# One power per half step, the third accumulator's load moved forward, and another order on TensorE around the verdict

## The reference

```
x = x + tanh(g0) * attention(layernorm(x), ctx, ctx)
h = layernorm(x)                                   # first feed-forward, 1024 wide
z = h @ ternary(W_syn).T + b_syn
hidden = where(z >= 102nd largest z of the row, relu(z), 0)
x = x + tanh(g1) * layernorm2(h + hidden @ ternary(W_out).T + b_out)
kv = k * v ; y = causal convolution of kv with a 256-long kernel, + D * kv
x = x + tanh(g2) * sum over i of y[i, j] * layernorm(x)[i]     # 16 heads of 8
n = layernorm(x)                                   # second feed-forward
x = x + tanh(g3) * (top-6-of-64 expert mixture(n) + shared expert(n))
```

## Time and profile before

| what | value |
|---|---|
| three timed runs | 716.46 us median (712.61 to 722.75) |
| the profiled execution | 720.17 us, of which the span is 718.4 us |
| mean granted TensorE clock of the span | 0.944 |
| busy: PE, PEld, DVE, ACT, POOL | 611.0, 470.5, 471.6, 296.9, 451.8 us |
| chain that ended last, by engine | PE 57%, DVE 14%, issue 11%, POOL 9%, DMA 6% |

### The profile page before, as it was taken

How to read it: one execution, slowest core, us unless ns; L and a number is a source line. 1 busy time by engine, 2 the same in 40 slices (tenths; PEclk the granted TensorE clock), 3 DMA queues, 4 the chain that set the end, 5 groups by cost and what they waited for, 6 DMA issues and landing times.

```text
span 718.4 us, 11813 instructions
## 1 busy us (share of the span) xinstructions
PE 611.0 (85%) x3072; PEld 470.5 (65%) x3072; DVE 471.6 (66%) x1596; ACT 296.9 (41%) x657; POOL 451.8 (63%) x512
## 2 busy tenths in 40 slices
PE   4789998769788798989857879999999999999920
PEld 2455554446566677877746668888888888878710
DVE  5898987999259988898895534444454454544515
ACT  3157777958233454555455223322233232323200
POOL 2697845782022287878787724777777777786560
PEclk9799999989899999999989899999999999999965
DMA  7579715869959943953333768999999999996878
GB/s 243 181 255 317 258 46 186 231 181 304 317 195 376 373 160 130 309 203 115 150 109 129 237 217 209 240 284 256 281 249 284 258 263 278 264 271 105 231 122 295
DMA packets 97822, 163.69 MB, mean 228 GB/s; under 512 B 10848, under 2 KB 65568, under 8 KB 96736
## 3 DMA queue, kind: packets, MB, share of 16 engines
q1 hardware_dynamic: 76864, 135.16, 56.9%
q0 software_dynamic: 20608, 27.82, 20.2%
q10 hardware_dynamic: 288, 0.01, 0.0%
HBM read 91.24 MB, written 71.71 MB: 227 GB/s over the span
## 4 chain that ended last, share of the span: by engine, by line
PE 57%; DVE 14%; issue 11%; POOL 9%; DMA 6%; ACT 1%; SPq 1%; DVEq 0%; POOLq 0%; ACTq 0%
PE psum L1164 12%; PE psum L1177 7%; PE psum L1168 6%; PE psum L904 5%; POOL xs_rows L781 5%; PE psum L1182 4%; PE psum L1148 4%; PE psum L1048 3%; PE psum L978 3%; PE psum L946 3%; PE psum L947 3%; PE psum L948 2%; DMA acc<-hh,toki 2%; POOL acc L847 2%; DVE Z L1962 1%
## 5 line engine op out<-in xcount | busy, mean ns | idle before, releaser
L847 POOL DMA_INDIRECT acc<-hh,toki x128 | 187.9, 1468 | 80.4 <-DVE hh L2173 40.9
L2173 DVE TENSOR_SCALAR hh<-psum,wtok 96x256 f32<-96x256 f32 (+3 forms) x128 | 55.8, 478 | 131.8 <-issue 110.7
L781 POOL DMA_INDIRECT xs_rows<-Z,slot x96 | 101.6, 1058 | 33.5 <-issue 23.4
L1481 ACT ACTIVATE qT<-psum 128x384 f32<-128x384 f32 (+3 forms) x64 | 33.5, 524 | 91.9 <-PE psum L1148 91.0
L694 POOL TENSOR_TENSOR rstd<-mv,neghalf 128x1 f32<-128x1 f32 x48 | 32.4, 685 | 59.9 <-DVE mv L1920 41.5
L978 PE MATMUL psum<-wt,hh 128*128 128x256 f32 x256 | 59.2, 385 | 4.5 <-DVE mv L1920 3.4
L904 PE MATMUL psum<-wt,hTs 128*128 128x512 f32 x128 | 59.7, 609 | 0.6 <-ACT hTs L1260 0.6
L978 PEld LDWEIGHTS psum<-wt,hh 128*128 128x128 f32 x256 | 48.0, 192 | 11.3 <-ACT hh L1355 4.6
L1164 PE MATMUL psum<-qT,kve 128*128 128x192 f32 (+3 forms) x256 | 52.8, 350 | 0.0
L1048 PE MATMUL psum<-Z,wt 128*128 128x256 f32 (+1 forms) x192 | 48.7, 406 | 0.8 <-DVE H L2035 0.8
L1487 ACT ACTIVATE H<-psum 128x192 f32<-128x192 f32 (+3 forms) x64 | 22.2, 348 | 63.7 <-PE psum L1164 62.0
(11 more groups left out here) (368 smaller groups left out, 1434.9 us busy)
## 6 DMA issues: line engine op xcount, KB each, us to landing
xs_rows<-fill SPq DMA_DIRECT2D x64, 272.0 KB, 4.5
kve<-in_wexp SPq DMA_DIRECT2D x32, 496.0 KB, 4.1
Z<-in_wexp SPq DMA_DIRECT2D x30, 496.0 KB, 4.3
kve<-co_rows SPq DMA_DIRECT2D x8, 1376.0 KB, 7.5
kv_rows<-Z SPq DMA_DIRECT2D x8, 688.0 KB, 3.9
kve<-kv_rows SPq DMA_DIRECT2D x8, 688.0 KB, 7.9
Z<-xs_rows SPq DMA_DIRECT2D x24, 204.0 KB, 4.2
Z<-xs_rows SPq DMA_DIRECT2D x16, 272.0 KB, 3.1
```

The source lines that it names most:

```text
L781: pool.indirect_dma_start(out=xs_rows[:, :], out_offset=bass.IndirectOffsetOnAxis(ap=slot[:, t, k:k + 1], axis=0), in_=H[:, t, :], in_offs ...
L847: pool.indirect_dma_start(out=acc[a][:, :], out_offset=bass.IndirectOffsetOnAxis(ap=toki[0:p, g, j:j + 1], axis=0), in_=y_sb[0:p, s, j, :] ...
L2173: m = dve.tensor_scalar(y_sb[0:p, s, j, :], pY[par][0:p, j * D:(j + 1) * D], wtok[0:p, g, j:j + 1], None, ALU.mult)
```

## The change

1. POOL takes one power over two neighbouring columns (`var4` of tile b - 1 and `var3` of tile b) after waiting for both, and makes `shift` in one instruction in place of two. ACT's query and DVE's centring wait for these.
2. `ALT` goes from 54 to 51, so that expert 50 is the last of the third accumulator and experts 51 to 53 go to the second, first and second. SP loads the third accumulator in the last turn of the `refill` loop, between the rows of experts 59 and 60, in place of after the overflow loop's loads.
3. PE sums the verdict ahead of `conv(13)` in place of behind it; `conv(14)` goes behind the first projection and `conv(15)` behind the second. ACT copies them out in the same order. A projection waits until the `residual` of the tile before has been read from bank 0, no longer for that tile's `var3`.

```diff
-    ALT = 54
+    ALT = 51
@@ sync
+            def load_third():
+                sp.wait_ge(added[2], sums_of(2, E))
+                for c in range(4):
+                    sp.dma_start(third[c], acc_lines[2][:, 4 * c:4 * c + 4, :]).then_inc(early_in, 16)
+
             def refill(i, near, far, groups):
                 for g in range(0, WS, 2):
+                    if g >= groups and g == WS - 2:
+                        load_third()
                     for j in range(2):
                         next_rows(WS * i + 6 + g + j, (g + 2 + j) % 4, near if g < 2 else far)
...
-            sp.wait_ge(added[2], sums_of(2, E))
-            for c in range(4):
-                sp.dma_start(third[c], acc_lines[2][:, 4 * c:4 * c + 4, :]).then_inc(early_in, 16)
             sp.wait_ge(added[1], sums_of(1, E))
@@ gpsimd
             def norm_pows(b):
 
+                t = b - 1
+                lo_, hi_ = max(t, 0), min(b + 1, NT)
                 if b < NT:
-                    pow_tile(b, var3_ready, rstd3_ready)
-                t = b - 1
+                    pool.wait_ge(var3_ready, b + 1)
                 if 0 <= t:
-                    pow_tile(t, var4_ready, rstd4_ready)
-                    pool.wait_ge(rstd4_ready, 3 * t + 1)
-                    pool.tensor_tensor(shift[:, t:t + 1], mv[:, t, 0:1], rstd[:, t:t + 1], ALU.mult).then_inc(rstd4_ready, 1)
-                    pool.wait_ge(rstd4_ready, 3 * t + 2)
-                    pool.tensor_tensor(shift[:, t:t + 1], eps2[:, 0:1], shift[:, t:t + 1], ALU.subtract).then_inc(rstd4_ready, 1)
+                    pool.wait_ge(var4_ready, t + 1)
+                pool.tensor_tensor(rstd[:, lo_:hi_], mv[:, lo_:hi_, 1], neghalf[:, lo_:hi_], ALU.pow).then_inc(rstd3_ready, 1)
+                if 0 <= t:
+                    pool.wait_ge(rstd3_ready, t + 2)
+                    pool.tensor_scalar(shift[:, t:t + 1], mv[:, t, 0:1], rstd[:, t:t + 1], -1.0, ALU.mult, ALU.mult).then_inc(rstd4_ready, 1)
@@ tensor
-            for k in range(AHEAD):
+            for k in range(AHEAD - 1):
                 conv(k)
-            pe.wait_ge(co_ready, AHEAD)
+            pe.wait_ge(co_ready, AHEAD - 1)
             pe.wait_ge(bad_ready, 1)
             pe.matmul(psum[:, 0, 0:1], onesf[:, :], bad[:, :], start=True, stop=True).then_inc(ones_done, 1)
+            conv(AHEAD - 1)
@@ project(b)
                 if b:
-                    pe.wait_ge(var3_ready, b)
+                    pe.wait_ge(hid_made, b + 2)
@@ tensor, the first step
-            conv(AHEAD)
             turn_hidden(0)
             turn_hidden(1)
             project(0)
-            conv(AHEAD + 1)
+            conv(AHEAD)
             for v_ in range(NPAIR):
...
                 project(2 * v_ + 1)
+                if v_ == 0:
+                    conv(AHEAD + 1)
@@ scalar
-                act.wait_ge(rstd4_ready, 3 * b + 3)
+                act.wait_ge(rstd4_ready, b + 1)
...
-            keep_conv(AHEAD)
             evac_hidden(0)
             evac_hidden(1)
-            keep_conv(AHEAD + 1)
+            keep_conv(AHEAD)
             for v_ in range(NPAIR):
...
                     evac_hidden(2 * v_ + 2)
+                if v_ == 0:
+                    keep_conv(AHEAD + 1)
@@ vector: residual raises hid_made, and the sum over its rows waits for that
-                return mark(dve.scalar_tensor_tensor(H2[:, b, :], psum[:, 0, 0:D], wsc[:, 1:2], H2[:, b, :], ALU.mult, ALU.add))
+                dve.scalar_tensor_tensor(H2[:, b, :], psum[:, 0, 0:D], wsc[:, 1:2], H2[:, b, :], ALU.mult, ALU.add).then_inc(hid_made, 1)
```

More of the change, by code:

```diff
@@ L1926, in second_block @@
                 if tile:
-                    at_h = residual(b, b % 2)
+                    residual(b, b % 2)
                 if behind:
@@ L1932, in second_block @@
                 if tile:
-                    at_h = row_sums(H2[:, b, :], NT, at_h)
+                    dve.wait_ge(hid_made, b + 3)
+                    alone(dve, "dve")
+                    at_h = mark(dve.bn_stats(stats[:, NT, :], H2[:, b, :]))
                 if behind:
```

## The result

The change makes the kernel slightly slower: 722.38 us against 718.48 us (medians of 20 runs each), a ratio of 1.006 with a 95% interval of 1.0039 to 1.0082, or +4.3 us (2.8 to 5.9). 712.1 was forecast, and the measured time lies above the top of the range (720). The sign is wrong too: the loss is small, but beyond the measurement's uncertainty. Of the kernel before, twenty runs have a median 2.0 us above that of the three (716.46) that the forecast starts from.

A forecast was written before the change was run, and what follows sets the result against it. The prediction took a chain of waits, 57% on PE, with different limits at the three changed places. Ramp -1.7, powers -0.3 and tail -2.4 made -4.4 on 720.17, 715.8; less 3.7 for that run's excess over the median, 712.1, range 704 to 720.

The forecast's parts named there:

- the ramp's "Gain: 214.76 - 213.0 = 1.7 us": Ahead of stage two: times_q(0) starts at 213.0, when group 0 lands, in place of 214.76; gain 1.7 us.
- What was saved is spent on putting two projections ahead: Ramp on PE: first projection ends 7.8 us sooner, yet conv(15) ends at 201.6, as before (201.66).
- The estimate of 8.8: Store and load of group 0 behind conv(15): 3.6 plus 5.2 us by the skill's formula, against the rows' 9.9.
- The clock, taken at nothing: PE idling while DVE waits for the load could take back between 0 and 1.7 us; 0 was taken.
- Powers: POOL's half steps: 0 in the steady steps, one instruction less in the final scatters, -0.3 us.
- The wait of the projection: Projections on PE waiting for residual in place of var3: 0, at most 1.7 us.
- The branch: Ramp: the number's load and DVE's branch behind hide, taken as 1.1 us, at most 5.0.
- Tail: Earlier third load and ALT 51: between a gain of 2.8 and a loss of 0.8 us; -2.4 taken.
- the forecast's cases: Tail, waits of experts 51 to 53: 2.1 us loses nothing; one slow landing (5.0) 0.7, two (7.9) 3.6.
- the late start: Rival, chance 0.12: at the ramp the branch takes 5.0 us, the next convolution runs at half clock; 719.4 us.
- A tail that gives nothing: Rival, chance 0.18: slow landings among experts 51 to 54 eat the idle, expert 60 starts unchanged; 714.5 us.
- a POOL that paces the steps: Rival, chance 0.08: POOL sets the steady steps' pace, 1.05 us more saved in each of some ten half steps; 701.6.

The follow-up runs named there:

- e1: Kernel before with only the merged power and single shift per half step on POOL; ratio 1.0011 (0.9987 to 1.0035).
- e2: Kernel before with only the tail part: ALT 51 and the third load in refill's last turn; ratio 0.9953 (0.9923 to 0.9983).
- e7: Kernel before with the merged power, but shift in three small instructions in place of one; its one run took 722.83 us.
- e8: Kernel before, unedited, profiled a second time; 714.11 us, span 712.4.
- e11: The whole change, unedited, profiled a second time; 35.4 us from the copy of conv(12) to times_q(0).
- e3: Kernel before with only the new order of verdict, conv(14) and conv(15), without the projection's new wait; ratio 1.0057 (1.0027 to 1.0087).
- e4: The changed kernel with the powers part undone: two powers and two shifts again; ratio 1.0039 (1.0014 to 1.0063) against before.
- e9: The changed kernel with only the order on PE and ACT undone; ratio 0.9976 (0.9944 to 1.0009) against before.
- e5: Kernel before with only the verdict moved ahead of conv(13); ratio 1.0064 (1.0026 to 1.0103).
- e10: Kernel before with only the projection's wait changed from var3 to residual of the tile before; ratio 0.9982 (0.9946 to 1.0018).
- e6: Kernel before with only conv(14) put behind the first and conv(15) behind the second projection; ratio 1.0105 (1.0055 to 1.0156).

## Why the prediction was wrong

**The step that failed is the ramp's "Gain: 214.76 - 213.0 = 1.7 us".** Its second number held (213.3 on that scale). Its first, the `times_q(0)` of before, came from an execution in which `conv(14)` stood 1.7 us and then ran at half clock. In the four other profiles with the order and the wait of before (e1, e2, e7, e8) it is 32.4 to 32.8 us behind the copy of `conv(12)`, against 37.0. The whole path of the change (35.5, 35.4) is shorter than 37.0 and longer than 32.6: -1.7 becomes +2.8. The prediction's own row said so: at 188 the clock was 0.50, and the step put `conv(14)` at 3.47 on the change's side without asking whether before also had it at 3.47 as a rule. And it took the 3.7 us by which this execution stood above the median of three runs off the sum, as if they lay spread over the kernel; 4.4 us (37.0 - 32.6) lay just where the edit was. The path came out step by step as forecast; that it looked 1.7 us shorter than before's was an accident of one execution.

**The mechanism behind it was there.** "What was saved is spent on putting two projections ahead": against a before whose `conv(14)` runs at the full clock the earlier verdict saves nothing, and `conv(15)` ends 4.3 us later (23.7 against 19.4), which is the second projection with its transposes that now stand ahead of it, 3.47 + 0.87. DVE had 1.7 us of room there; the other 2.6 are about the 2.8. Store and load themselves took 4.54 + 5.80 = 10.3 us behind the copy (9.9 in the forecast). The estimate of 8.8 that the prediction set beside it, by the Trainium skill, "DMA: Bandwidth & Descriptors", section "Anatomy of one DMA — SWDGE (gpsimd) path", is further off.

**The clock, taken at nothing, costs 1.7 us** in the first profile of the change (first step 25.73 against 24.05) and 3.0 in the second. "Between 0 and 1.7" was the bound; the first lies at its upper end, the second beyond it. The reason given, that DVE has the first work behind the load, didn't cover PE's matmuls at 221 and 248 us, over which the chain runs. The long first step stands in all four profiles with the whole order (the change, e11, e3, e4), but also in e9 without it, and in none of the other eight. In those five PE had stood 2.2 to 3.2 us ahead of that place, in the eight at most 1.55. So it goes with the order, which is not its only cause. The section of the Trainium skill that was cited as speaking against the change ("TensorE: Matmul & The Clock Gate", "HAM oscillation — how this bites in real kernels") is borne out by the windows at 222 and 248 us, behind waits of PE.

**Powers:** -0.3 forecast, +0.8 (-0.9 to +2.5) measured. That POOL does not set the pace held; that its time is then free did not: `mask` pays 0.23 us in each middle step. The -0.3 was to come from the last burst of scatters, and no run shows it: from the first scatter of the sixth pair to the last one it is 47.8 us in e1 and in the change, but also with two powers in e3, e5 and e10, and 48.2 in e11 with one.

**The wait of the projection:** 0, as forecast (e10). **The branch:** 1.1 us were taken for it; in e6 PE starts 0.1 us after `hide` ends (185.03 + 2.47 = 187.50 to 187.61). Little hung on it, as the sum started the first projection only 0.3 us late for it.

**Tail:** -2.4 forecast, -3.4 (-5.5 to -1.2) measured; from the last scatter of stage two to the last adding scatter, the five profiles with the new tail (the change, e11, e2, e4, e9) take 274.0 to 276.6 us (mean 275.2), the eight with the old one 275.7 to 279.1 (277.5): -2.3. The waits of 51, 53 and 54 were 6.1 us, between the 5.0 and 7.9 of the forecast's cases, and POOL's later idle took nearly all of them.

**The rivals:** the late start had 0.12 and the right sign, by luck. Its branch took 0.1 us and not 5.0, and its mark, an end of `conv(15)` after about 206, was not met: on the prediction's scale it is 201.5 in the change, and 205.1 (177.79 + 27.3) in e3 and e4, where PE stood for `bad`. A tail that gives nothing is refuted by e2, and a POOL that paces the steps by steps that became longer, not shorter.

**The sum now:** +2.8 at `times_q(0)`, +1.7 to +3 for the clock, +0.9 for the powers (0.23 in four steps), -2.3 for the tail: +3.1 to +4.4, beside the measured 2.8 to 5.9. It takes the full clock in `conv(14)` as the rule for before, by four profiles of which e8's (714.11) is itself 4 us below before's median. What stays open: e5 is slower by 1.9 us at least, while its one profile shows 1.7 at `times_q(0)` and no long first step. How often an execution meets the wait for `bad`, the slow `conv(14)` or the long first step is not known from one or two profiles each, and so the loss is not settled term by term.

Of all these edits, e2, the tail alone, is the only one shown to gain: 0.47% faster than before (0.17 to 0.77).

## What to carry to other kernels

Before a stretch is costed from one profile, ask whether something in it is an accident of that execution: a clock of 0.50 or a wait of unnamed cause inside the very stretch that an edit moves may not be there the next time, and a profile that stands above the median has its excess somewhere. A second profile of the unedited kernel, like e8, shows whether it is. Work moved ahead of a result pushes back whatever hangs on that result: follow the last store that a load waits for, not the engine that gets busier. Look for what covers each wait before moving work: moving half of a reordering can open a wait that the other half had closed. And two engines that don't wait for each other by semaphore can still meet, as `mask` and the scatter do here.

## What had not been expected of the hardware

`mask` on DVE takes twice its time (0.46 against 0.23) when it begins 0.6 us into a POOL scatter of 1.06 us, ending with it, and its normal time when it begins 0.1 us into one. In e7, delaying POOL's scatter by half a microsecond gives DVE the 0.23 us back in each middle step; that the kernel gets faster by it is not shown.
